# A four-layer conditioned transformer on one core: the score stage in four batches inside the MLP part, projection halves between single transposed pairs, and the causal mask in VectorE's row maximum

## The reference

```
h = norm1(x) * (1 + scale1) + shift1
q, k, v = h @ Wqkv (+ b)                        # 16 heads of 16 features
s = q @ k.T / 4                                 # per head, 256 x 256
L1 only:  s = where(tril, s, -inf)              # causal
L3 only:  q, k = rope(q), rope(k) before s
x = x + gate1 * (softmax(s) @ v @ Wproj + b)
h = norm2(x) * (1 + scale2) + shift2
x = x + gate2 * (act(h @ W1 + b1) @ W2 + b2)    # act: exact gelu, hidden width 1024
                                                # L3: a * silu(gate), W1 is twice as wide, no gates on x
```

## Time and profile before

| | |
|---|---|
| median of three runs | 2399.96 us |
| profiled execution, its time | 2402.53 us |
| its span | 2400.7 us, 63280 instructions |
| TensorE busy | 2240.4 us, 93% |
| VectorE busy | 1660.3 us, 69% |
| ScalarE busy | 1254.3 us, 52% |
| GpSimd busy | 1089.8 us, 45% |
| granted TensorE clock, mean | 0.989 |

### The profile page before, as it was taken

How to read it: one execution, slowest core, us unless ns; L and a number is a source line. 1 busy time by engine, 2 the same in 40 slices (tenths; PEclk the granted TensorE clock), 3 DMA queues, 4 the chain that set the end, 5 groups by cost and what they waited for, 6 DMA issues and landing times.

```text
span 2400.7 us, 63280 instructions
## 1 busy us (share of the span) xinstructions
PE 2240.4 (93%) x20392; PEld 1859.2 (77%) x20392; DVE 1660.3 (69%) x3866; ACT 1254.3 (52%) x2620; POOL 1089.8 (45%) x1333
## 2 busy tenths in 40 slices
PE   7699999999999999999999999999999999999997
PEld 5477887778777877877877777777778787888877
DVE  3567666677666556556677666766788888888873
ACT  0366556656554554555566555656564434444442
POOL 1244454445444444444554444444554454444433
PEclk9899999999999999999999999999999999999998
DMA  6221112212221121122232112112222212121210
GB/s 210 92 70 61 59 62 68 68 59 74 84 84 54 58 68 50 58 68 64 77 107 70 56 60 70 61 56 69 72 89 64 66 54 70 53 70 51 72 54 14
DMA packets 164960, 166.12 MB, mean 69 GB/s; under 512 B 29329, under 2 KB 144401, under 8 KB 164849
## 3 DMA queue, kind: packets, MB, share of 16 engines
q1 hardware_dynamic: 164848, 164.69, 21.5%
HBM read 58.47 MB, written 4.39 MB: 26 GB/s over the span
## 4 chain that ended last, share of the span: by engine, by line
PE 58%; issue 14%; POOL 10%; DVE 9%; ACT 4%; SPq 1%; POOLq 1%; DMA 0%; DVEq 0%; ACTq 0%
PE B L482 25%; PE B L587 8%; PE B L741 6%; PE B L530 5%; PE B L716 5%; POOL GHl L1244 5%; PE B L507 3%; PE B L596 3%; ACT PR L890 3%; DVE NEGM L961 3%; PE B L606 1%; POOL H1l L1289 1%; POOL X L1230 1%; PE B L689 1%; DVE HF L1087 1%
## 5 line engine op out<-in xcount | busy, mean ns | idle before, releaser
L890 ACT ACTIVATE PR<-B 128x512 f32<-128x512 f32 (+1 forms) x1024 | 506.7, 564 | 339.1 <-PE B L716 230.6
L1244 POOL TENSOR_TENSOR GHl<-G,GHh 128x256 fp32r<-128x256 f32 x512 | 378.0, 739 | 481.8 <-ACT GHh L863 327.6
L961 DVE TENSOR_REDUCE NEGM<-B 128x2 f32<-128x512 f32 x768 | 477.7, 683 | 61.2 <-PE B L530 60.4
L482 PE MATMUL B<-H2h,W1h 128*128 128x256 f32 x1280 | 394.8, 308 | 3.2 <-issue 3.1
L863 ACT ACTIVATE G<-B,VEC 128x256 f32<-128x256 f32 x384 | 182.1, 474 | 359.5 <-PE B L482 356.9
L482 PE MATMUL B<-H2h,W1l 128*128 128x256 f32 x1280 | 362.9, 283 | 0.0
L482 PE MATMUL B<-H2l,W1h 128*128 128x256 f32 x1280 | 362.4, 283 | 0.0
L587 PE MATMUL B<-W2h,GHh 128*128 128x256 f32 x1024 | 299.3, 292 | 3.5 <-POOL GHl L1244 3.5
L741 PE MATMUL B<-PR,V 128*32 128x256 f32 (+1 forms) x4096 | 261.3, 373 | 36.3 <-ACT PR L890 29.4
L587 PE MATMUL B<-W2l,GHh 128*128 128x256 f32 x1024 | 289.5, 283 | 0.0
L587 PE MATMUL B<-W2h,GHl 128*128 128x256 f32 x1024 | 288.8, 282 | 0.0
(11 more groups left out here) (148 smaller groups left out, 4813.2 us busy)
## 6 DMA issues: line engine op xcount, KB each, us to landing
QS<-QHL SPq DMA_DIRECT2D x768, 64.0 KB, 2.1
KS<-KHL SPq DMA_DIRECT2D x768, 64.0 KB, 2.1
GA<-gate_scratch SPq DMA_DIRECT2D x48, 256.0 KB, 3.2
GM<-gate_scratch SPq DMA_DIRECT2D x48, 256.0 KB, 3.3
RAW<-in_w SPq DMA_DIRECT2D x36, 256.0 KB, 3.2
CW<-in_cw SPq DMA_DIRECT2D x3, 1536.0 KB, 13.7
X<-in_x SPq DMA_DIRECT2D x2, 2048.0 KB, 10.2
QS<-MT SPq DMA_DIRECT2D x256, 4.0 KB
```

The costliest lines, as they stand in the source:

```text
L482: last = nc.tensor.matmul(dst, w[i], x[j], start=(first_k and n == 0), stop=(last_k and n == 2))
L890: nc.scalar.activation(PR[:, h % PRING].rearrange("p k q -> p (k q)")[:, 0:n], src[:, 0:n], ACT.Exp, scale=SCALE).then_inc(ac_exp, 1)
L961: last = nc.vector.tensor_reduce(NEGM[:, :, c], src, op=ALU.max, axis=AX.X, negate=True)
L1244: nc.gpsimd.tensor_tensor(GH[1][:, j % RING, :], G[:, j % RING, :], GH[0][:, j % RING, :].bitcast(F32), ALU.subtract).then_inc(po_gl, 1)
```

## The change

1. The score stage starts earlier. Pairs 0 and 1 stand behind the transpose of the attention outputs and ahead of `up(4)`, pairs 2 and 3 behind the output projection, 4 and 5 behind `down(4)`, 6 and 7 behind `down(6)`. It uses banks 4, 5, 0, 1 (the last pair 0 and 2), so the output projection and norm 1's transpose move to bank 6, and `query` waits until the last maximum of bank 1 is taken.
2. The first row of maxima is transposed ahead of `up(7)`, and ScalarE copies it after its hidden tile 6.
3. `query(0)`, `query(1)`, `key(0)` and `key(1)` alternate with the transposed pairs 0 to 3. `values(0)` stands behind `outputs(0)`, `values(1)` between `outputs(2)` and `outputs(3)`. Norm 2's transpose stands behind `outputs(1)` in all layers.
4. L0 to L2 get norm 1 of the next tile in the MLP part of the same step, as L3 had it; its statistics on VectorE move from the end of a step to its front.
5. VectorE takes the maxima in the order of the batches, the first head's ahead of `outputs_lo` and the next three's behind it. In L3 `rotate` of k stands ahead of `modulate_2`, and GpSimd's sum for k ahead of H2l.
6. In L1 the score stage has no mask matmul. VectorE's `tensor_tensor_reduce` adds the mask (bf16, in SBUF) to the scores, writes the sum back to PSUM and reduces it, in place of a `tensor_reduce`.

```diff
-S_BANKS = (4, 5, 0, 6) * 2 + (4, 5, 0, 2) * 2
-WO_BANK = 1
+S_BANKS = (4, 5, 0, 1) * 3 + (4, 5, 0, 2)
+WO_BANK = 6
+NORM1_BANK = 6
...
                     if s.la == CAUSAL:
+                        apart(dv)
                         for i in range(NT):
-                            last = nc.vector.tensor_reduce(NEGM[:, i, c:c + 1], src[:, i, 0:(i + 1) * P],
-                                                           op=ALU.max, axis=AX.X, negate=True)
+                            keys = (i + 1) * P
+                            unmasked = MASK[:, 0].rearrange("p b c -> p (b c)")[:, T - keys:T]
+                            last = nc.vector.tensor_tensor_reduce(src[:, i, 0:keys], src[:, i, 0:keys], unmasked, -1.0,
+                                                                  HIGHEST, ALU.add, ALU.min, NEGM[:, i, c:c + 1])
...
-                    if s.la == CAUSAL:
-                        for h in (2 * p, 2 * p + 1):
-                            mask(0, banks[h]).then_inc(pe_s, 1)
...
                 if s.r is not None:
                     outputs_to_features()
+                scores_if(0)
+                scores_if(1)
                 up_if(4)
                 down_if(2)
                 if s.r is not None:
                     output_projection()
-                scores_if(0)
-                scores_if(1)
+                scores_if(2)
+                scores_if(3)
                 up_if(5)
                 down_if(3)
-                if rope:
+                if s.q is not None:
                     norm_1()
                 up_if(6)
                 down_if(4)
-                scores_if(2)
-                scores_if(3)
-                up_if(7)
...
                 scores_if(4)
                 scores_if(5)
-                down_if(7)
                 if scored:
                     maxima_to_rows(0)
-                query(0)
-                query(1)
+                up_if(7)
+                down_if(5, 6)
                 scores_if(6)
                 scores_if(7)
-                key(0)
-                key(1)
-                if s.a is not None:
+                down_if(7)
+                query(0)
+                if scored:
                     transposed_pair(0)
+                query(1)
+                if scored:
                     transposed_pair(1)
                     maxima_to_rows(1)
-                    values(0)
+                key(0)
+                if scored:
                     transposed_pair(2)
-                    if not rope:
-                        values(1)
+                key(1)
+                if scored:
                     transposed_pair(3)
                     outputs(0)
+                    values(0)
                     transposed_pair(4)
-                    if s.r is not None and not rope:
-                        norm_2()
                     transposed_pair(5)
                     outputs(1)
-                    if s.r is not None and rope:
+                    if s.r is not None:
                         norm_2()
                     transposed_pair(6)
                     transposed_pair(7)
                     outputs(2)
-                    if rope:
-                        values(1)
+                    values(1)
                     outputs(3)
```

More of the change, by code:

```diff
@@ L502, in body, with mask @@
             def body(s):
-                def mask(transposed, n):
-                    dst = B[:, n, :].rearrange("p (b c) -> p b c", b=4)[:, 0:4 - transposed:3 - transposed, :]
-                    return nc.tensor.matmul(dst, IDENTB[:], MASK[:, transposed], start=False, stop=True,
+                def mask(n):
+                    dst = B[:, n, :].rearrange("p (b c) -> p b c", b=4)[:, 0:3:2, :]
+                    return nc.tensor.matmul(dst, IDENTB[:], MASK[:, 1], start=False, stop=True,
                                             skip_group_check=True)
@@ L519, in score_pair @@
                         pe.wait_ge(dv_max, H * a_ + max(b for b in before if b is not None) + 1)
-                    if before[1] is None and banks[2 * p + 1] == 6:
-                        at_least(pe, ac_ot, s.r_done)
-                        at_least(pe, dv_ot, s.r_done)
+                    if before[1] is None and banks[2 * p + 1] == 1:
+                        at_least(pe, dv_on, 2 * s.r_done)
+                        at_least(pe, dv_q, s.nq)
                     elif before[1] is None and banks[2 * p + 1] == 2:
@@ L722, in transposed_pair @@
                         for h in (2 * p, 2 * p + 1):
-                            mask(1, banks[h]).then_inc(pe_st, 1)
+                            mask(banks[h]).then_inc(pe_st, 1)
                 def outputs(g):
@@ L918, in modulate_1 @@
                 for f in range(KD):
-                    last = nc.scalar.activation(HF[:, f, :], bank(1)[:, f, :], ACT.Identity,
+                    last = nc.scalar.activation(HF[:, f, :], bank(NORM1_BANK)[:, f, :], ACT.Identity,
                                                 bias=cond(s, s.lq, s.sq, C_B1 + f), scale=cond(s, s.lq, s.sq, C_S1 + f))
@@ L1011, in statistics_1 @@
                 def statistics_1(tile, sequence, layer):
-                    if isinstance(tile, int) and tile == 4:
+                    if isinstance(tile, int) and tile == 3:
                         dv.wait_ge(sp_x[1], 16)
@@ L1057, in body @@
                     multiply(s, bank(7), GM, sp_gm, s.m, s.lm).then_inc(dv_dn, 1)
-                maxima(6)
+                maxima(7)
                 def statistics_2():
@@ L1109, in values_out @@
                     nc.vector.tensor_copy(VT[:], bank(2)).then_inc(dv_v, 1)
-                maxima(7)
                 statistics_2()
@@ L1132, in body @@
                     modulate_2()
-                    if s.n is not None and s.ln != ROPE:
-                        statistics_1(s.n, s.sn, s.ln)
                     evacuate(0)
-                    if s.n is not None and s.ln != ROPE:
-                        normalise_1(s.n, s.sn, s.ln, s.q_done)
                     values_out()
@@ L1245, in body @@
                                                 ALU.subtract).then_inc(po_gl, 1)
-                    if j == 2 and s.lq == ROPE:
+                    if j == 2 and s.q is not None:
                         rstd(MV1, RS1, TV1, dv_mv1, po_t1, po_rs1, s.q, s.lq)
@@ L1251, in body @@
                         residual_1(s)
[L1252 removed]
+                    if j == NJ - 2:
                         low_1(s)
[L1254 to L1255 removed]
                 if s.m is not None:
@@ L1272, in body @@
                     nc.gpsimd.tensor_tensor(H2[1][:], HF[:], H2[0][:].bitcast(F32), ALU.subtract).then_inc(po_h2, 1)
-                if s.n is not None and s.ln != ROPE:
-                    rstd(MV1, RS1, TV1, dv_mv1, po_t1, po_rs1, s.n, s.ln)
-                if s.lq == ROPE:
-                    r = s.q - NSEQ * ROPE
-                    po.wait_ge(dv_rot, 2 * r + 2)
-                    nc.gpsimd.tensor_tensor(GK[:, 0:KD, :], GK[:, 0:KD, :], GK[:, KD:2 * KD, :], ALU.add).then_inc(po_rot, 1)
                 if s.q is not None:
@@ L1436, in lay_out @@
     mask = np.zeros((P, 2, NT, P), np.float32)
-    mask[:, 0] = np.where(col > row, MASKED, 0.0)[:, None]
+    mask[:, 0, NT - 1] = np.where(col > row, MASKED, 0.0)
     mask[:, 1] = np.where(row > col, MASKED, 0.0)[:, None]
```

87 lines of the change are left out of this document (47 added, 40 removed).

## The result

The changed kernel takes 2313.89 us (median of four runs, 2312.17 to 2315.45) against 2398.93 for the kernel before on the same chip: ratio 0.9643, 95% interval 0.9626 to 0.966, 85 us off. The profiled span is 2310.6 us where it was 2400.7; TensorE is busy in 95% of it (before 93%), VectorE in 74% (69%).

A forecast was written before the change was run, and what follows sets the result against it. A step was TensorE's list plus its waits, in L3 VectorE's order. Savings of 12 (L0), 30 (L1), 26 (L2) and 3 (L3) make 71 us; from the profiled 2402.5 that gives 2331, as a median 2329, range 2300 to 2395.

The forecast's parts named there:

- likeliest case: The forecast itself, 2329 us for the whole kernel, chance 0.55, own range 2310 to 2350 us.
- TensorE's list: TensorE's matmuls in one step: 12 interruptions of the 128-row products instead of 11, +0.2 us, bounds 0 to 0.6.
- Waits: TensorE's idle time left per step: 0.35 us before pair 2, 0.2 before the last outputs, 0.1 for small ones.
- c: VectorE's time per head for L1's new maximum with its result reads: 0.72 us, from 0.55 to 1.40.
- The room of 0.73: L1, first batch to second transpose of maxima: 11.7 us for 16 heads; each 0.1 above 0.73 costs 1.6 a step.
- the unevenness: L1 step: 0.5 us added because every batch waits for the maxima of the one before, with four banks.
- The two rules on c: Two Trainium skill sections on VectorE in L1: the first gives about 1.03 us a head, the second lets unheld instructions overlap.
- No cover left: L3's stacked keys KS land about 8.5 us into the step, the first batch stands at about 8.6; counted as just enough.
- Series reads: Rival, VectorE in L1: each read waits for its reduction's end, 1.03 us a head, 2398 us in all; chance 0.14.
- a slow stream: Rival, VectorE in L1: the new operation streams slowly, 1.40 us a head, 2492 us in all; chance 0.07.
- L3's loss of order: Rival, L3: up(7) is late by 1.5 us, 26 us more, 2355 us in all; chance 0.12.
- The waits only move: Rival, L0 and L2: ScalarE's stall costs what the last outputs saves, 35 us more, 2364 in all; chance 0.12.

The follow-up runs named there:

- e3: Changed kernel with TensorE's attention part in its old order (both halves of q and k ahead of the transposed pairs): 2313.92 us, ratio 0.9643.
- e7: Changed kernel with q's halves in one block ahead of pairs 0 and 1, k's in one behind the second transpose of maxima: 2285.22 us.
- e1: Kernel before with part 6 alone, the new maximum that adds the mask on VectorE in L1: 2370.36 us, ratio 0.9883.
- e2: Changed kernel without part 6: mask matmuls and plain reduction back in L1, the new order kept: 2353.83 us, ratio 0.9813.
- e8: Changed kernel with ScalarE copying the second row of maxima after its second exponential instead of its first: 2291.72 us, ratio 0.9543.
- e9: Changed kernel with the edits of both e7 and e8: 2275.56 us, ratio 0.9489.
- e10: e9 with key(0) and key(1) also ahead of pair 0, so q and k form one block: 2397.58 us, ratio 0.9998.
- e5: Changed kernel with three more one-column copies on VectorE behind each head's maximum in L1: 2324.85 us, ratio 0.9682.
- e6: Changed kernel with VectorE taking pair 5's maxima ahead of hidden tile 7 in L3 instead of behind it: 2312.97 us, ratio 0.9642.
- e4: Changed kernel with score pairs 0 and 1 behind the output projection and their maxima behind outputs_lo: 2528.19 us, ratio 1.0545.

## Why the prediction was right

2329 us was forecast, 2313.9 came, inside the likeliest case's own range. Step by step:

- *TensorE's list.* +0.2 us a step was forecast. Measured are +0.05 in L0 and +0.5 in L3. The added interruptions cost what was forecast, 0.20 (e3) to 0.26 (e7) against 0.18; in L1 it was less, 0.04 (e7) to 0.15 (e3). The two merged ones were counted at 0.18 as well and gave 0.28 each in L0 (e3 against before).
- *Masks.* -2.7 forecast, -2.3 (e1) to -2.5 (e2) measured.
- *Waits.* 0.65 was forecast as left in L0 and L2, 0.38 is. The part of it that I named, ScalarE's copy ahead of its second exponential, is right in place and size (0.32 against 0.35, and e8 removes it), though 0.31 stood there before the change already. The 0.2 before the last `outputs` is 0. So L0 is 32.17 and not 32.6, L2 32.31 and not 32.6.
- *Why the waits go.* I put it down to the projection halves between single pairs. e3 shows that this is true of the wait before the last `outputs` and false of the time: what it takes off the waits it pays in TensorE's list. Most of the gain of L0 and L2 comes from the front of the step, from merged interruptions and from waits (for H1l, for norm 2's input) that the prediction did not name. So its total for these two layers is near in part by luck. k in one block behind the second transpose of maxima and `values(1)` ahead of the last `outputs` are enough to cover the exponentials in L0 and L2 (e7, e9); without k's block they are not (e10).
- *L1 and c.* c was forecast at 0.72 and is 0.62. I had priced the read of the result at half of a small instruction; in the chain it costs nothing. The room of 0.73 was right (e5). L1 is 33.00 and not 34.0, and its list is as forecast (32.78 against 35.32 - 2.7 + 0.2 = 32.82). Two terms were too large: the unevenness, 0.5, which is 0, and the 0.65 of waits carried over from L0, of which 0.21 is there; the kernel before had only 0.57 in L1.
- *The sum.* By the steps, 1 to 15 saved 6.3 us more than forecast, 16 to 31 11.4, 32 to 46 2.5, step 47, L3 and the two ends 3.5, and steps 48 and 49 took 4.5: 19 together, 90 between the profiled spans against 71. Between the medians it is 15.
- *The two rules on c.* Both operations' lengths and both reads add up to 0.461 + 0.314 + 2 x 0.137 = 1.05 us, and a head takes 0.62. The Trainium skill, "VectorE: DVE Perf Modes", section "The DRAIN you can't avoid", says that the next operation does not start until the pipe is empty, by which c would have been that sum, and adds that one that is not held starts earlier. The prediction left the addition out. The same page, section "Two Vector instructions with no wait between them", says which instructions are held, and that an accumulator output is written by a read that is judged by itself. The trace agrees with the addition, for the accumulator's read too: it starts at 929.93, before its operation's end at 930.00.
- *Norm 2.* 0.3 us of cover was forecast, and H2l stays covered: no wait stands before `up(0)` in L0.
- *L3.* -0.2 forecast, -0.05 measured. VectorE comes to hidden tile 7 1.0 us later in the step (0.9 forecast) and takes 14.2 from there to HF's end (13.9 forecast), so HF ends where it ended. But HF still waits 0.39 for norm 2's transpose, so its time hangs on TensorE's list as well: e7, whose list is 0.55 shorter in L3, takes 0.45 off the step, and filling 0.81 us of VectorE's idle time takes 0.13 (e6). "No cover left" for KS is right in the steady steps, since no wait for the DMA shows there.
- *Layer borders.* "Steps at layer borders count as unchanged" is wrong. In steps 48 and 49 the MLP is still of single width and the stacked keys already come in L3's late order, so the first batch waits 2.13 and 1.69 us, and the clock falls behind it: +4.5 us (+2.5 in e5, where it did not fall). The cover that I worked out for L0 and for L3 is the cover of neither here. Steps 17 and 18 save 1.4 each and not 1.9, by the wait behind the split of new weights.
- *Rivals.* Series reads, a slow stream and L3's loss of order did not come. *The waits only move* is in part what happened to the interleaving: its gain was lost in TensorE's list, not in another wait.

## What to carry to other kernels

Interleave short foreign matmuls with wide products only where a wait stands: in L0, L2 and L3 each such interruption costs 0.2 to 0.28 us whether it hides something or not. So keep the products in blocks, and place as few blocks as cover the waits. Price a wait of TensorE not by its length alone: behind waits of 1.5 to 2.5 us a step the clock was in most steps at half for some microseconds, which made them cost 1.5 to 2.5 times their length. When transfers are made earlier or their readers are, count the cover for the border steps too, in which the layers' widths mix or new weights are split.

## What the runs showed of the hardware that I had not expected

- The granted clock falls behind waits that are short beside a step. After 1.24 + 0.69 us (e4) it was 0.50 for some 7 us and cost 2.7 us, after 0.80 + 0.70 (e10) 1.5. The same waits in the same layer's steps did it in most of them and not in others, and one of 2.13 did it where one of 2.09 did not (step 48 of the changed kernel and of e5); what decides between them stays open.
- Reading out the accumulator (0.137 us each, 512 of them) takes none of VectorE's time in a chain.
- A one-column copy of 0.15 us, behind others of its kind, takes 0.06 to 0.07.
